# Row scores of two heads in two neighbouring PSUM banks with one maximum over both; tasks and column scores in one ring of three banks

## The reference, cut to what matters

```python
mod = (_silu(L0_c) @ L0_wmod).reshape(8, 6, 1, -1)          # sa, ca, ga, sb, cb, gb
h = _layernorm(x) * (1 + ca) + sa                           # x: 8 x 512 x 128
q, k, v = split(h @ w_qkv)                                  # 16 heads of 8 channels
attn = softmax(q @ k.T / sqrt(128))                         # per batch and head: 512 x 512
x = x + ga * ((attn @ v) @ w_out)
h = _layernorm(x) * (1 + cb) + sb
x = x + gb * moe(h)                                         # 8 experts, top 2
```

## Time and profile before

| | |
|---|---|
| median of 3 runs | 685.91 us (685.17 to 688.14) |
| profiled execution, span | 679.4 us |
| PE busy | 618.9 us (91%) |
| DVE busy | 550.1 us (81%) |
| ACT busy | 450.5 us (66%) |
| POOL busy | 267.2 us (39%) |
| DVE maxima (L864), 512 of 683 ns | 323.0 us busy |
| ACT exponentials (L656), 512 of 599 ns | 270.8 us busy |

### The profile page before, as it was taken

How to read it: one execution, slowest core, us unless ns; L and a number is a source line. 1 busy time by engine, 2 the same in 40 slices (tenths; PEclk the granted TensorE clock), 3 DMA queues, 4 the chain that set the end, 5 groups by cost and what they waited for, 6 DMA issues and landing times.

```text
span 679.4 us, 13009 instructions
## 1 busy us (share of the span) xinstructions
PE 618.9 (91%) x3413; PEld 285.7 (42%) x3413; DVE 550.1 (81%) x1065; ACT 450.5 (66%) x859; POOL 267.2 (39%) x384
## 2 busy tenths in 40 slices
PE   5299999999999999999999999889899999999995
PEld 3112223323323322322322322225667777777773
DVE  3698889899888988988988988714788888888885
ACT  2107878778778778778778777876554555555553
POOL 4522022222222222222122122333567776776773
PEclk9658999999999999999999999979899999999999
DMA  7703505304304304303403400253334454345411
GB/s 183 197 31 82 183 3 117 106 20 106 117 19 95 126 17 95 127 17 79 143 18 72 150 18 4 76 167 109 92 114 139 137 142 141 130 137 150 136 35 31
DMA packets 48972, 65.58 MB, mean 97 GB/s; under 512 B 9432, under 2 KB 30432, under 8 KB 48928
## 3 DMA queue, kind: packets, MB, share of 16 engines
q1 hardware_dynamic: 46304, 64.32, 33.1%
q10 hardware_dynamic: 2624, 0.79, 0.5%
HBM read 47.26 MB, written 17.83 MB: 96 GB/s over the span
## 4 chain that ended last, share of the span: by engine, by line
PE 34%; DVE 20%; issue 19%; POOL 16%; ACT 5%; DMA 2%; SPq 1%; DVEq 1%; POOLq 0%; ACTq 0%
POOL hid_lo L612 13%; DVE negmax L864 13%; PE o_acc L1172 11%; PE s_row L1149 10%; PE s_col L1162 5%; ACT probs L656 3%; DVE probs L1042 1%; POOL h_lo L618 1%; PE misc L1130 1%; PE misc L1103 1%; PE misc L1100 1%; SPq L325 1%; DVE sums_inv L883 1%; DVE k_rest L878 1%; PE misc L1126 1%
## 5 line engine op out<-in xcount | busy, mean ns | idle before, releaser
L864 DVE TENSOR_REDUCE negmax<-s_row 128x1 f32<-128x512 f32 x512 | 323.0, 683 | 47.5 <-PE s_row L1149 41.9
L656 ACT ACTIVATE probs<-s_col 128x512 f32<-128x512 f32 x512 | 270.8, 599 | 76.4 <-PE s_col L1162 73.4
L1149 PE MATMUL s_row<-k_stack,q_stack 64*128 64x512 bf16 x512 | 141.7, 402 | 25.2 <-DMA k_stack<-k_scr 11.6
L612 POOL TENSOR_TENSOR hid_lo<-probs,hid_hi 128x512 fp32r<-128x512 f32 x87 | 128.5, 1493 | 61.9 <-ACT hid_hi L800 61.9
L1162 PE MATMUL s_col<-q_stack,k_stack 64*128 64x512 bf16 x512 | 132.4, 383 | 7.1 <-ACT probs L656 6.5
L1172 PE MATMUL o_acc<-probs,v_aug 128*32 128x512 f32 x1024 | 138.1, 612 | 0.0
L800 ACT ACTIVATE hid_hi<-probs 128x512 fp32r<-128x512 f32 x88 | 55.6, 632 | 85.0 <-DVE probs L1042 84.6
L1149 PEld LDWEIGHTS s_row<-k_stack,q_stack 64*128 64x128 bf16 x512 | 34.9, 93 | 180.1 <-DVE negmax L864 142.1
L1042 DVE TENSOR_TENSOR probs<-probs,q_stack 128x512 f32<-128x512 f32 x56 | 62.5, 1116 | 15.7 <-POOL hid_lo L612 13.6
L520 POOL CAST negmax_parts<-negmax 128x16 bf16<-128x16 f32 x32 | 6.3, 196 | 163.0 <-DVE negmax L864 163.0
L1032 DVE TENSOR_TENSOR probs<-probs,s_col 128x512 f32<-128x512 f32 x88 | 59.6, 677 | 2.9 <-ACT probs L820 1.6
(11 more groups left out here) (134 smaller groups left out, 713.9 us busy)
## 6 DMA issues: line engine op xcount, KB each, us to landing
q_scr<-q_parts SPq DMA_DIRECT2D x48, 128.0 KB, 2.4
k_scr<-k_parts SPq DMA_DIRECT2D x48, 128.0 KB, 2.4
q_stack<-q_scr SPq DMA_DIRECT2D x8, 768.0 KB, 6.1
k_stack<-k_scr SPq DMA_DIRECT2D x8, 768.0 KB, 7.5
q_stack<-combT_scr SPq DMA_DIRECT2D x24, 256.0 KB, 3.4
k_stack<-combT_scr SPq DMA_DIRECT2D x16, 224.0 KB, 2.9
q_stack<-combT_scr SPq DMA_DIRECT2D x16, 192.0 KB, 2.7
q_stack<-combT_scr SPq DMA_DIRECT2D x16, 160.0 KB, 2.6
```

Source lines behind the costliest of these rows:

```text
L612: nc.gpsimd.tensor_tensor(hid_lo[k % HIDDEN][:], weighed[(par + k) % 2], hid_hi[k % HIDDEN][:], ALU.subtract).then_inc(s["hid_split"], 1)
L656: nc.scalar.activation(probs[t % 2][:, j, :], s_col[score_bank("col", u)][:], ACT.Exp, scale=INV_SCALE).then_inc(s["exp_done"], 1)
L864: nc.vector.tensor_reduce(negmax[n % 2][:, j, qc:qc + 1], s_row[score_bank("row", u)][:], AX.X, ALU.max, negate=True).then_inc(s["row_max" ...
L1149: nc.tensor.matmul(s_row[score_bank("row", u)][:], q_stack[par][at:at + KS, head // 2, P * qc:P * (qc + 1)], k_stack[par][at:at + KS, head ...
```

## The change

Banks: `s_row` becomes two pairs of neighbouring banks (four banks), `ring` has three banks, `o_acc` keeps its one, and `misc` is gone.

Row scores: both heads of a half go into the two banks of one pair, with one semaphore increment on the second product. One DVE instruction takes both maxima (128 x 2 out of 128 x 2 x 512), 32 per batch where there were 64. Half-slot h waits for the maximum of half-slot h - 2. PE's order within a half is now row, row, column, column.

Ring: column scores and tasks take the banks of `ring` in turn, in PE's order (`ORDER`, 64 units and 17 tasks, 81 places, a multiple of three). Whoever writes place p waits (`ring_free`) for the reader of place p - 3, whatever that is: an exponential, or a task's evacuation. A task that the first or the last batch leaves out keeps its place, and the wait goes to the place three further back. `REST` moves: `q_rest` and `k_rest` now stand behind the maximum of the whole half 1 of slots 1 and 2. In the block stage the banks have other names and the same number.

```diff
-    TURN = {"row": G * (1 + AHEAD) + 2, "col": G * 1 + 2}
+    ORDER = []
+    for t in range(SLOTS):
+        for half in range(2):
+            ORDER += [G * t + 2 * half, G * t + 2 * half + 1]
+            if (t, half) in TASKS:
+                ORDER.append(TASKS[t, half])
+        if (t, 2) in TASKS:
+            ORDER.append(TASKS[t, 2])
...
-        s_row = [bank(f"s_row{i}") for i in range(SCORES)]
-        s_col = [bank(f"s_col{i}") for i in range(SCORES)]
+        s_row = [ctx.enter_context(nc.psum_tensor(f"s_row{i}", [P, 2, N], F32)) for i in range(2)]
+        ring = [bank(f"ring{i}") for i in range(RING)]
         o_acc = bank("o_acc")
-        misc = bank("misc")
...
-                nc.vector.tensor_reduce(negmax[n % 2][:, j, qc:qc + 1], s_row[score_bank("row", u)][:], AX.X, ALU.max,
+                nc.vector.tensor_reduce(negmax[n % 2][:, 2 * half:2 * half + 2, qc], s_row[pair % 2][:], AX.X, ALU.max,
                                         negate=True).then_inc(s["row_max"], 1)
...
-            REST = {(1, 2): "q", (2, 2): "k"}
+            REST = {(1, 1): "q", (2, 1): "k"}
...
+                if not (isinstance(b, int) and b == 0 and pair < 2):
+                    pe.wait_ge(s["row_max"], ROW_PAIRS * b + pair - 1)
+                for i in range(2):
...
+            def ring_free(b, first, last, place):
+                mine = tasks(first, last)
+                while True:
+                    place = place - RING
+                    what = ORDER[place % PLACES]
...
+                    of = b if place >= 0 else b - 1
+                    if not isinstance(what, str):
+                        pe.wait_ge(s["exp_done"], UNITS * of + what + 1)
+                        return
+                    if place >= 0 and what in mine:
+                        free(owner(of, what), what)
+                        return
...
-                for t in range(SLOTS):
-                    def scores(j):
+                for t in range(SLOTS):
+                    for half in range(2):
                         if t < SLOTS - AHEAD:
-                            row_scores(b, par, t + AHEAD, j)
+                            row_scores(b, par, t + AHEAD, half)
...
-                            scores(j)
-                            col_scores(b, par, t, j)
+                            col_scores(b, par, t, j, first, last)
                         turn((t, half))
```

More of the change, by code:

```diff
@@ L1089, in free, with task @@
                     pe.wait_ge(s["combT_ready"], b + 2)
-            def task(b, par, name):
+            def task(b, par, name, ps):
                 if name == "xT":
@@ new lines, in row_scores @@
+                last.then_inc(s["row_ready"], 1)
+            def ring_free(b, first, last, place):
[3 more added lines that the diff above has]
+                    what = ORDER[place % PLACES]
+                    if place < 0 and first:
+                        if place % RING == RING - 1:
+                            free(0, "max0")
+                        return
[5 more added lines that the diff above has]
+                        free(owner(of, what), what)
+                        return
+                    if place < 0:
+                        assert what == "combT"
+                        pe.wait_ge(s["combT_ready"], b)
@@ L1154, in col_scores @@
+            def col_scores(b, par, t, j, first, last):
                 n, kc = t // CH, t % CH
```

196 lines of the change are left out of this document (92 added, 104 removed).

## The result

The kernel with the change takes **711.4 us** (median of four: 700.02, 709.19, 713.65, 714.01) against 685.7 us beside it on the same chip, 25.7 us more. Over its two quicker runs alone, since the other two fell to a lower granted clock, it takes 1.028 times as long as the kernel before (95% interval 1.020 to 1.036). The prediction's direction was right, its size was not: it said +9.2 us, and only the quickest of the four lies in the range. The profile is of the run of 714.01 us, with a span of 712.2 us and a mean granted clock of 0.933; that of the run of 700.02 us was 0.962. The profile before has a mean clock of 0.966, and with a span 1.8 us under the time of its run, as here, its 679.4 us belong to a run of some 681.2 us, not to the median. The two profiles therefore differ by 32.8 us, more than the medians do.

The account below looks back on a forecast made before the run. Bound: ACT through three column-score banks, right behind the DVE waits. Loop batches +6.0, batch 0 +2.4, batch 7 +1.9, prologue -1.1 make +9.2 us: span 688.6, plus 6.5 to the median, 695.1 us; range 688.0 to 701.5.

Parts of the forecast that it names:

- q_rest and k_rest: Slots 2 and 3: both stand before column scores, which start late; 0.29 and 0.42 us a loop batch.
- What bounds the kernel: Attention slots: freed of DVE, a plain slot gains only 0.02 to 0.03 us, as ACT through three column banks binds next.
- R1: Rival: DVE was the bound and the ACT loop has slack, so only gains of 9.6 us stand; 676.3 us, chance 0.07.
- R4: Rival: the pair's maximum costs two singles, 1.37 us instead of 1.21; 699.7 us, chance 0.05.
- DVE's busy time: Sign: with joined maxima DVE's busy time falls by some 18 us of 550 and its idle time grows by more.
- the prologue's saving: Prologue, where DVE is full: 16 joined maxima save 1.1 us.
- The ring's cost: Slots with a task behind half 0: unit 3 waits for unit 1's exponential instead of unit 0's; 1.77 us a loop batch.
- The list of tasks behind half 1: Router and max0 at (t, 1) were also said to wait for unit 1's exponential, 0.18 and 0.07 us.
- Slot 15's 0.46 falling into ACT's late start: Batches 3 and 5: ACT begins slot 0 a microsecond late anyway, hiding slot 15's 0.46; six loop batches cost 6.0, not 6.9.
- R2: Rival: costs and gains cancel, without the two stalls and with slightly larger gains in slots 2 to 6; 687 us, chance 0.12.
- R3: Rival: PE's three register instructions per half, where it had two, cost 0.04 us each half; 703 us, chance 0.06.
- ACT 10 us or more: Sign that the forecast is right: PE's waits of column scores for ACT grow by 10 us or more.

Follow-up runs that it names:

- experiment 2: Kernel before, with column scores of slots 2 and 3 waiting for q_rest and k_rest, both moved behind the fourth maximum: 697.2 us, ratio 1.012.
- experiment 7: Changed kernel with q_rest and k_rest between the two maxima of slots 1 and 2 instead of behind the second: 700.28 us, ratio 1.020.
- experiment 6: Changed kernel with each pair's maximum taken by two single instructions of 512 columns: 710.83 us, ratio 1.040.
- experiment 9: Changed kernel with q_rest and k_rest between the two maxima, and idle products in slots 8 to 15 of batch 7: 698.16 us, ratio 1.017.
- experiment 5: Changed kernel with 32 idle products, read by nobody, in slots 8 to 15 of batch 7: 703.8 us, ratio 1.028.
- experiment 10: Kernel before with the idle products in slots 8 to 15 of batch 7: 683.07 us, ratio 0.996.
- experiment 12: Ring of four banks with three single row banks, against the kernel before, plus the idle products in batch 7: 679.32 us, ratio 0.991.

## Why the prediction was right and wrong

In short: the direction and the kind of each cost were right, and the sum was too small. It took 0.9 us off in batches 3 and 5 that did not go, made q_rest and k_rest 0.2 us a batch too cheap, put nothing on slots 6 and 8 and too little on slot 12, and had no term for the clock.

**What bounds the kernel: right.** A plain slot freed of DVE gained 0.03 us, as read from the earlier trace rows; R1 fell with it. Slot 14 gained 0.56 and slot 7 0.27, to the hundredth. The pair's maximum took 1.22 us for 1.21, so R4 fell. DVE's busy time fell by 14 us (550.1 to 536.1), not by 18; the prologue's saving came (0.95 us of 1.1).

**The ring's cost: right in its mechanism, too small in two places, and slot 6 missed.** The subtractions from the earlier trace rows held in slots 4, 5, 11 and 15 (+0.30, +0.21, +0.17 and +0.47 for 0.29, 0.19, 0.18 and 0.46). The list of tasks behind half 1 was wrong by one: router and max0 were in it, max3 of slot 8 (0.15) was left out. And max0's wait cost 0.24, not 0.07. Slot 6, put at nothing, took 0.2 to 0.9 us more by ACT's wait for the store of the maxima. Slot 12 of batch 2:

```profile
200.06 0.39 PE L1172 MATMUL ring<-q_stack,k_stack 64*128 64x512 bf16 x1 [0.34 <-ACT probs L643]
200.75 0.22 PE L1095 MATMUL ring<-ident,negmax_parts 128*48 128x128 bf16 x1 [0.30 <-ACT probs L643]
```

**q_rest and k_rest: right in kind, 0.2 us small.** Slots 0 to 3 grew by 1.04 us for 0.84. Slots 2 and 3 of batch 4:

```profile
274.42 1.23 DVE L851 TENSOR_REDUCE negmax<-s_row 128x2 f32<-128x1024 f32 x1 [0.37 <-PE s_row L1137]
...
275.56 0.68 DVE L860 TENSOR_TENSOR q_rest<-ring,q_parts 128x512 f32<-128x512 f32 x1
...
276.27 0.63 ACT L651 ACTIVATE q_parts<-q_rest 128x512 bf16<-128x512 f32 x1 [0.35 <-DVE q_rest L860]
276.29 0.17 PEld L1172 LDWEIGHTS ring<-q_stack,k_stack 64*128 64x128 bf16 x2 [0.38 <-DVE q_rest L860]
...
277.12 1.09 ACT L643 ACTIVATE probs<-ring 128x512 f32<-128x512 f32 x2 [0.22 <-issue]
...
280.06 0.47 PE L1172 MATMUL ring<-q_stack,k_stack 64*128 64x512 bf16 x2
```

q_rest starts 1.14 us behind the pair's maximum (1.13 forecast), and the column scores of slot 2 start as it ends. But slot 1 gained only 0.20 of its 0.45, and behind q_rest ACT takes the middle part and issues a transfer before it gets to the exponentials: the first starts 0.82 us after its column scores at 276.30, where it otherwise starts 0.5 after. The prediction had that order of ACT and put 0.2 on it. Experiments 2 and 7 give these stalls 1.2 and 0.9 us a batch, the largest part after the ring (0.71 forecast).

**Slot 15's 0.46 falling into ACT's late start: wrong.** The 0.9 us subtracted for batches 3 and 5 weren't there. At the full clock slot 0 of these batches takes 4.4 to 4.7 us in experiments 6, 7 and 9, for 3.96 and 4.22 before: it grows like any slot 0. ACT at the start of batch 3, before and then after, with PE's wait:

```profile
204.01 1.08 ACT L656 ACTIVATE probs<-s_col 128x512 f32<-128x512 f32 x2 [1.30 <-PE s_col L1162]
```

```profile
212.58 1.09 ACT L643 ACTIVATE probs<-ring 128x512 f32<-128x512 f32 x2 [2.12 <-issue]
213.23 0.09 PEld L1172 LDWEIGHTS ring<-q_stack,k_stack 64*128 64x128 bf16 x1 [1.59 <-ACT probs L643]
```

ACT's lateness is not a due time that PE's delay could use up. It starts when ACT has finished slot 15, so it moves with slot 15: the exponentials of the last half end at 202.70 before and at 210.46 after, and the first of the batch starts 1.31 and 2.12 us after that. Between batches 3 and 4, where the loop does not go round, the same gap is 0.22 us before and 0.69 after: 0.47 more there too, slot 15's own cost.

**The missing term: the clock.** The sum took its rows from batch 4, where the clock is 1.00, and had no term for what the standing does to it. The profiled runs differ by 32.8 us. Worked out from the slots of the two traces: 6 loop batches x 1.70 at the full clock without slot 6 (10.2), slot 6's wait for the store of the maxima (2.3), batch 0 (2.1), batch 7 at the full clock as in experiment 5 (2.5), less 0.2 in slot 1 of batches 3 and 5: **16.9 us**. The slots that lie in low clock took 1.9 more in batch 0, 3.7 in batch 3, 1.1 in batch 4, 3.7 in batch 5 and 5.1 in batch 7: **15.5 us** (some 0.6 of it, in slot 0 of batches 3 and 5, is ACT's later start). Together 32.4, and 0.4 lies behind the attention stage. The 16.9 agree with the 18 us that the runs show at a like clock. The 15.5 do not stand for the kernels, only for these two profiles, whose mean clocks are 0.966 and 0.933; between the medians the clock is 6 to 8 us.

Against the 9.2 forecast, then, some 8 us are terms of the sum that were too small or missing, and the clock is 6 to 8 more. The former, from the two traces: 3.3 in slots 0 to 5, 8, 11 and 12 of the loop batches, 2.3 in slot 6, 0.9 wrongly taken off in batches 3 and 5, 0.6 in batch 7, and 1.1 of the prologue, whose rows began late in this run, less 0.5 in batch 0 and slot 1. The sum itself also leaves out the 0.2 that it takes off in batch 7. Its yardstick was too fine as well: it held that 0.5% can be told, but runs of the kernel before spread over 1.7% with the clock.

**R2 and R3.** R2 fell: the stalls are real. R3's 0.04 us in each half is not there: in slot 13 the groups of products follow each other at 0.22 us, and slots 13 and 14 take 2.67 and 2.68 us, as forecast from the ACT loop alone. The block stage is equal, as said. Of the signs named, "ACT 10 us or more" came as 68.

## What to carry to other kernels

When two kinds of work share a ring of buffers, go through the order and write down, for each place, whose reader stands a ring's length back: with three banks a task between products made the second next product wait for a reader that the old split never had, 0.15 to 0.47 us a slot where nothing hid it, and a fourth bank removed all of it. Relieving the engine with the most waits pays only as far as the wait right behind it, which one slot of the trace shows (0.03 us here). And compare runs at a like mean clock before reading a cause from them: here one and the same kernel spread over 11.6 us with it, and two profiles with mean clocks 0.033 apart made the clock look twice as costly as it was. Where TensorE stands a little more, let the range reach to its clock, here 6 to 8 us.

## What the runs showed of the hardware

- The granted clock fell to 0.50 for stretches of 3.4 to 27.3 us inside the attention stage, which the profiled run before spent at 1.00 but for 6.8 us behind batch 0's start. With 27.3 us of it instead of 6.8, batch 7 took 6.1 us more in experiment 2, in which its own instructions had not changed.
- 32 idle products kept batch 7 at 1.00 in all four kernels that had them (experiments 5, 9, 10 and 12), and raised the mean clock of their runs.
- The time of one and the same kernel follows its mean granted clock, within some 3 us. The kernel before took 680.9 us at 0.971, 685.5 at 0.961 and 692.0 at 0.942; the change 700.0 at 0.962 and 714.0 at 0.933.
- A slot without row scores takes 2.6 us at the full clock and 3.69 at half of it, so that it is PE's own work, not ACT's, that bounds it then.
- One maximum over two neighbouring banks works and costs 1.22 us, with the next 1.13 behind; two single ones cost 0.60 each. In the prologue, where DVE is full, 16 pairs saved 0.95 us; in slots 1 and 2 of a loop batch 0.06 us each.
- Where the hardware loop goes round, ACT computed nothing for 1.3 to 2.1 us between the last exponential of one pass and the first of the next.
- A 12 KB store issued behind three loads of SP let its reader go on 6.5 us after its issue; with one load ahead of it, it had landed after 3.1 us.
